# Reading a turned block from its bank, and writing expert results to token slots

## The chip, the cores and the metric

The kernel runs on one core of a Trainium2 chip. The metric is the device time of one launch in microseconds, here the median of three runs: 1955.56 us (1953.64 to 1967.84). PE is TensorE (matmuls, PEld its weight loads), DVE is VectorE, ACT is ScalarE, POOL is GpSimd, SP is SyncE. ACT and DVE read and write PSUM and SBUF; POOL issues the indirect DMAs and SP the plain ones.

## The reference, cut to what matters

Four layers, each a gated cross attention and a gated feed-forward part, work on x of 8 x 256 tokens with 256 features. Three of the four feed-forward parts (layers 0, 1, 3) route every token to two of eight experts. The one that most of the change is about is the last:

```python
def _L3_ffn_ref(x, gate_w, gate_bias, w1, w3, w2, sw1, sw3, sw2):
    scores = softmax(xt @ gate_w.T);  _, idx = top_k(scores + gate_bias, 2)
    weights = take_along_axis(scores, idx, axis=1)
    for e in range(8):
        gate_e = sum(where(idx == e, weights, 0.0), axis=1)
        h = silu(xt @ w1[e].T) * (xt @ w3[e].T)
        y = y + gate_e[:, None] * (h @ w2[e].T)
    z = silu(xt @ sw1.T) * (xt @ sw3.T) @ sw2.T      # two shared experts' width
    return (y + z).reshape(shape)
x = x + tanh(g_ffn[3]) * _L3_ffn_ref(_layernorm(x), ...)
```

Layers 0 (gelu, one shared expert) and 1 (relu, none) have the same form with biases. Layer 2's feed-forward part is not routed.

## The kernel before

**Routed layer.** `find_rows` picks the two experts of each of the 2048 tokens, sorts the 4096 pairs by expert into blocks of 256 rows (`BLOCKS` = 23, the rest is padding), and makes two tables: `token_of`, from a row of a block to its token, and `rows`, from a pair (token, choice) to its row. `routed_experts` then works block by block.

For each block b: POOL gathers its 256 token rows from the DRAM tensor `normed_x` with two indirect DMAs of 128 rows (L1673) into `block_rows`; PE turns them (four transposes, L1719) into PSUM bank 6 or 7; ACT copies the bank to `block_T` in full precision (L1784) and to `block_h`, rounded (L1785); DVE subtracts the two into `block_l` (L1893), the low part. The weights w1 and w2 are split the same way into high and low parts. PE makes the hidden products with three terms (L1699), 24 matmuls of 256 columns for a unit of 512 hidden columns; ACT and DVE make the hidden values and their high and low parts; PE makes the result products (L1709), 12 matmuls in layer 3, whose silu-gated unit is 256 wide, 24 in the others. The result is taken from its banks into `result`, which has two buffers, by ACT in layer 3 (L1601) and by DVE in layers 0 and 1 (L1604), and SP stores it to the DRAM tensor `sorted_y` (L1645), 256 KB.

**Order.** Each engine has its own hand-written queue, and `run` unrolls the first and the last bodies and loops over the ones between. PE's body(b) is: hidden products of b+1, turn of b+2, result products of b. ACT's body(b) in layer 3 is: silu of b, `take(b+1)` (the two copies), high part of the hidden values, high part of w1 (b+2), result of b-1, high part of w2 (b+1). DVE's is: `gated` (silu times the other half, L1849), `split_block(b+1)` (the low part), low parts of the hidden values, of w1 and of w2. In layers 0 and 1 DVE rounds the hidden values and subtracts their low part ahead of `split_block`. PE turns a block only when the low part of the block two before is made, or, before the change, when its high part is.

**Tail of layer 3.** Four batches' shared experts are computed beside the routing (HEAD), four after the blocks (TAIL), two units each: 16 hidden matmuls (L1699) and 8 result matmuls (L1709) a unit. PE runs one unit ahead: the hidden products of unit j+1 come before the result products of unit j, which need unit j's `gated` values from DVE. Meanwhile POOL waits for the last store to `sorted_y`, then issues 32 indirect gathers (L1686) of 128 rows, one for each of 16 tiles and two choices, into a ring of 16 pieces of the w1 buffers. DVE adds each to x with its gate (`combine`, L1937), in groups: after the shared result of batch 4 (L1855) it does 4, after batch 5 it does 8, after batch 6 it does 8 and after batch 7 the last 12. `store_output` (L1658) stores a batch of x when its combines and its shared result are done.

Of the kernel before, what the change touches and what calls it, by code (L numbers as in the profile page):

```python
# [18 lines left out]
I32 = mybir.dt.int32  # L19
# [90 lines left out]
def build(nc, dram, out, stages):  # L110
    with ExitStack() as whole:

        in_use = []

        def sem(name):
            in_use.append(nc.alloc_semaphore(name=name))
            return in_use[-1]

        def clear_semaphores():

            nc.clear_and_free_semaphores(in_use)
# [22 lines left out]
        codes = resident("codes", [P, 2 * TILES])  # L144
# [6 lines left out]
        env = dict(nc=nc, context_w=context_w, homes=homes, dram=dram, sem=sem, psum=psum, x=x, ident=ident, half=half, zero=zero, half32=half32, ctxT=ctxT, tg=tg,  # L151
                   rank=rank, stats=stats, mv=mv, var=var, rstd=rstd, before=before, ones=ones, counting=counting,
                   marks=marks, codes=codes)
        if any(kind == "f" and FFN[n].get("routed") for kind, n in stages):
            env["normed_x"] = nc.dram_tensor("normed_x", (TOKENS, D), F32, kind="Internal").ap()
            env["sorted_y"] = nc.dram_tensor("sorted_y", (BLOCKS * BLOCK, D), F32, kind="Internal").ap()
        env["context_ready"] = False
        env["out"] = out
        env["g_all"] = g_all
        attentions, expert_layers = stages[0::2], stages[1::2]  # L160
        assert all(kind == "a" for kind, n in attentions) and all(kind == "f" for kind, n in expert_layers)
        for (_, a), (_, f), following in zip(attentions, expert_layers, [n for kind, n in attentions[1:]] + [None]):
            with ExitStack() as pair:
                front = front_part(env, pair, f)
                with ExitStack() as scope:
                    attention_layer(env, scope, a, front)
                clear_semaphores()
                with ExitStack() as scope:
                    ffn_layer(env, scope, f, following, front)
                clear_semaphores()  # L170
            env["context_ready"] = True
# [770 lines left out]
def ffn_layer(env, scope, n, following, front):  # L942
# [8 lines left out]
    if routed:  # L951
        t["xn_all"] = front["xn_all"]
        t["gates"] = sb("gates", [P, TILES, cfg["experts"]])
        t["rows"] = sb("rows", [P, 2 * TILES], I32)
# [14 lines left out]
    with nc.Block() as block:  # L969
        @block.sync  # L970
        def _(sp):
            r_sync(sp)
            e_sync(sp)
            if ahead:
                t["operands_left"](sp)
                ahead["load_late"](sp)
            else:
                t["store_output"](sp)
# [75 lines left out]
def find_rows(env, scope, n, t):  # L1054
# [8 lines left out]
    def sb(nm, shape, dt=F32):  # L1063
# [3 lines left out]
        "consts", "chain", "shifted", "exped", "coded", "same", "summed", "table_done", "chosen", "counted",  # L1067
# [18 lines left out]
    t.update({k: sems[k] for k in ("rows_done", "blocks_done", "table_done")}, exponentials=choose.exponentials)  # L1086
# [31 lines left out]
    def place_rows(dve, step):  # L1118
# [29 lines left out]
        nc.vector.tensor_copy(t["rows"][:], rows_f[:].rearrange("p k t -> p (k t)")).then_inc(sems["rows_done"], 1)  # L1148
# [101 lines left out]
def experts(env, scope, n, t):  # L1250
# [205 lines left out]
    t.update(operands_left=operands_left, banks_left=banks_left, stated=stated, rows_places=rows_places)  # L1456
# [14 lines left out]
def routed_experts(env, scope, n, t):  # L1471
# [9 lines left out]
    xs, ys = env["normed_x"], env["sorted_y"]  # L1481
# [12 lines left out]
    COMBINED = (1, 7) if shared == 1 else (4, 12, 20)  # L1494
# [5 lines left out]
    own = own_follows(n)  # L1500
    RING = 8 if own else 16
# [16 lines left out]
    block_T = [sb(f"block_T{s}", [P, DC, BLOCK]) for s in range(2)]  # L1518
# [6 lines left out]
    gathered = [w1[j // 4][:].rearrange("p c i -> p (c i)")[:, j % 4 * D:(j % 4 + 1) * D] for j in range(RING)]  # L1525
# [33 lines left out]
    def run(engine, body):  # L1559
# [3 lines left out]
        for b in range(DEPTH):  # L1563
            body(b, 0, b, max(DEPTH, 3))
        with engine.Fori(1, rounds) as i:
# [42 lines left out]
    def sync(sp):  # L1608
        if own:
            t["ahead"]["load_early"](sp)  # L1610
        for s in range(2):
            sp.dma_start(ys[s * BLOCK:s * BLOCK + P, :], env["ctxT"][:, 0, 0:D]).then_inc(sems[f"stored{s}"], 16)

        def weights(b, s, freed):
# [3 lines left out]
            for u, unit in enumerate(units):  # L1618
# [3 lines left out]
                sp.dma_start(w1[k][:], dram[f"{name}_w1"][unit]).then_inc(sems[f"w_in{k}"], 16)  # L1622
                sp.dma_start(w2[k][:], dram[f"{name}_w2"][unit]).then_inc(sems[f"w_in{k}"], 16)
# [26 lines left out]
        run(sp, body)  # L1650

# [12 lines left out]
    def gpsimd(pool):  # L1664
# [3 lines left out]
        for b in range(BLOCKS):  # L1668
# [7 lines left out]

        for s in range(2):
# [14 lines left out]
    def tensor(pe):  # L1692
# [192 lines left out]
    def vector(dve):  # L1885
# [43 lines left out]
        def combine(j):  # L1929

            tile, k = divmod(j, 2)
            dve.wait_ge(sems[f"gathered{j % RING}"], 16 * (j // RING + 1))
# [4 lines left out]
            nc.vector.scalar_tensor_tensor(x[:, tile, :], gathered[j % RING],  # L1937
# [26 lines left out]
        for k, b in enumerate(TAIL):  # L1964
# [29 lines left out]
    def banks_left(pe):  # L1994
        pe.wait_ge(sems["hidden_out"], UNITS * OUT + HIDDEN0)
        pe.wait_ge(sems["result_out"], RESULTS + RESULT0)
        pe.wait_ge(sems["turned_out"], BLOCKS + 2)

    t.update(operands_left=operands_left, banks_left=banks_left, stated=stated, rows_places=rows_places)
# [137 lines left out]

# [741 lines left out]
```

## Time and profile before

| what | us |
|---|---|
| median of three runs | 1955.56 |
| the profiled execution, and its span | 1955.66, 1953.9 |
| PE busy, DVE busy, ACT busy, POOL busy | 1734.4, 1263.3, 974.7, 528.9 |
| blocks of layer 0 (first gather to last gather's end) | 207.4 to 359.6 |
| blocks of layer 1 | 808.6 to 1044.4 |
| blocks of layer 3 (first turn to last result) | 1760.6 to 1892.3 |
| tail of layer 3 (shared units after the blocks, to the end) | 1891.6 to 1953.9 |

The span runs from the first to the last instruction of the core. The execution's own time lies 1.8 us above it. Busy times of engines overlap; what an engine's work costs is read from whether another engine's queue stood still for it.

### The profile page before, as it was taken

The numbers are of one execution on the slowest core, as the hardware profiler recorded it, in microseconds if no ns is written. First come the engines' busy times: TensorE is split into PE (matmuls) and PEld (weight loads), VectorE is DVE, ScalarE is ACT, GpSimd is POOL, SyncE is SP. The second block draws the span as 40 slices with busy tenths as digits, with TensorE's granted clock in tenths as the row PEclk, the third lists the DMA queues.
The fourth block names the chain that finished last, engine by engine and source line by source line (L and its number), as shares of the span: only waits on it lengthen the run. The fifth ranks groups of instructions, "written<-read, shape, count | busy, mean of one in ns | idle before, by whom it ended". The sixth has DMA issues, their size and how long they took to land. (4 is left out here: it accounts for less than half of the span.)

```text
span 1953.9 us, 32441 instructions
## 1 busy us (share of the span) xinstructions
PE 1734.4 (89%) x11744; PEld 1436.2 (74%) x11744; DVE 1263.3 (65%) x2312; ACT 974.7 (50%) x1739; POOL 528.9 (27%) x492
## 2 busy tenths in 40 slices
PE   6998899987799997599999969999699699798896
PEld 4667799932577776599999648887588466588885
DVE  6886488646355563588888557665545688656644
ACT  4652366523676772277777225444353355316750
POOL 2320343264333332122221450000200244203334
PEclk9998799998799997599999979999699999889998
DMA  3003378520100000567676240000000100025743
GB/s 112 15 20 105 126 254 257 148 79 0 50 1 12 7 12 25 195 217 245 232 233 217 65 130 1 1 1 1 28 1 11 48 12 12 31 76 177 238 148 110
DMA packets 97907, 178.64 MB, mean 91 GB/s; under 512 B 25888, under 2 KB 62650, under 8 KB 96682
## 3 DMA queue, kind: packets, MB, share of 16 engines
q1 hardware_dynamic: 86264, 146.32, 22.8%
q0 software_dynamic: 11232, 30.69, 5.4%
q8 instruction: 76, 1.25, 0.3%
q14 instruction: 47, 0.39, 0.1%
q10 hardware_dynamic: 288, 0.00, 0.0%
HBM read 149.70 MB, written 27.26 MB: 91 GB/s over the span
## 5 line engine op out<-in xcount | busy, mean ns | idle before, releaser
L1673 POOL DMA_INDIRECT f_block_rows_home<-normed_x,f_token_of_sb x138 | 168.6, 1221 | 452.3 <-PE psum L1719 325.8
L1699 PE MATMUL psum<-f_block_h_sb,f_w1h_home 128*128 128x256 f32 x736 | 211.4, 287 | 29.8 <-DVE f_block_l_sb L1893 12.0
L1699 PE MATMUL psum<-f_block_h_sb,f_w1l_home 128*128 128x256 f32 x736 | 206.9, 281 | 0.0
L1699 PE MATMUL psum<-f_block_l_sb,f_w1h_home 128*128 128x256 f32 x736 | 206.8, 281 | 0.0
L2322 PE MATMUL psum<-a_xT_home,context_w 128*128 128x256 f32 x704 | 181.2, 403 | 13.6 <-PEq L122 9.7
L1709 PE MATMUL psum<-f_w2h_home,f_hidden_h_home 128*128 128x256 f32 x644 | 187.4, 291 | 1.8 <-DVE f_result_sb L1604 0.9
L1709 PE MATMUL psum<-f_w2h_home,f_hidden_l_home 128*128 128x256 f32 x644 | 181.8, 282 | 0.0
L1709 PE MATMUL psum<-f_w2l_home,f_hidden_h_home 128*128 128x256 f32 x644 | 181.7, 282 | 0.0
L1699 PEld LDWEIGHTS psum<-f_block_h_sb,f_w1h_home 128*128 128x128 f32 x736 | 141.0, 192 | 38.1 <-issue 28.2
L2487 ACT ACTIVATE a_probsT_sb<-psum 77x1024 f32<-77x1024 f32 (+1 forms) x128 | 130.8, 1022 | 71.4 <-PE psum L2374 69.0
L2322 PEld LDWEIGHTS psum<-a_xT_home,context_w 128*128 128x128 f32 x704 | 131.6, 197 | 45.0 <-issue 20.0
L1801 ACT ACTIVATE f_hidden_sb<-psum,f_b_sb 128x256 f32<-128x256 f32 x276 | 115.7, 471 | 78.2 <-PE psum L1699 76.7
L2374 PE MATMUL psum<-identity,a_probs_sb 128*77 128x128 f32 (+1 forms) x1024 | 141.7, 280 | 11.4 <-DVE a_inv_sb L2662 9.1
L2374 PEld LDWEIGHTS psum<-identity,a_probs_sb 128*77 128x77 f32 (+1 forms) x1024 | 116.1, 142 | 47.2 <-DVE a_inv_sb L2662 19.2
L2414 PE MATMUL psum<-a_wo_sb,a_attT_sb 128*128 128x256 f32 x640 | 145.3, 383 | 2.6 <-ACT a_attT_sb L2509 1.4
L1699 PEld LDWEIGHTS psum<-f_block_l_sb,f_w1h_home 128*128 128x128 f32 x736 | 141.1, 192 | 0.0
L1699 PEld LDWEIGHTS psum<-f_block_h_sb,f_w1l_home 128*128 128x128 f32 x736 | 140.8, 191 | 0.0
L2414 PEld LDWEIGHTS psum<-a_wo_sb,a_attT_sb 128*128 128x128 f32 x640 | 120.2, 192 | 19.1 <-ACT a_attT_sb L2509 2.3
L1686 POOL DMA_INDIRECT f_w_sb<-sorted_y,f_rows x96 | 93.1, 970 | 129.7 <-DMA sorted_y<-f_result_sb 95.3
L1709 PEld LDWEIGHTS psum<-f_w2h_home,f_hidden_h_home 128*128 128x128 f32 x644 | 122.8, 191 | 2.7 <-DVE f_hidden_l_home L1893 2.6
L1709 PEld LDWEIGHTS psum<-f_w2l_home,f_hidden_h_home 128*128 128x128 f32 x644 | 123.0, 191 | 0.0
L1709 PEld LDWEIGHTS psum<-f_w2h_home,f_hidden_l_home 128*128 128x128 f32 x644 | 122.8, 191 | 0.0
(310 smaller groups left out, 3929.8 us busy)
## 6 DMA issues: line engine op xcount, KB each, us to landing
f_w_sb<-in_f_w SPq DMA_DIRECT2D x161, 512.0 KB, 4.8
sorted_y<-f_result_sb SPq DMA_DIRECT2D x69, 256.0 KB, 2.3
normed_x<-f_xn_all SPq DMA_DIRECT2D x24, 256.0 KB, 2.1
f_b_row_sb<-in_f_b SPq DMA_DIRECT2D x46, 128.0 KB, 3.6
f_w_sb<-in_f_w SPq DMA_DIRECT2D x23, 256.0 KB, 4.0
f_block_rows_home<-normed_x,f_token_of_sb POOLq DMA_INDIRECT x138, 4.2
residual<-in_x SPq DMA_DIRECT2D x8, 256.0 KB, 6.2
context_w<-in_a_wk SPq DMA_DIRECT2D x2, 1024.0 KB, 5.2
```

What stands on the lines that cost most here:

```text
L1673: nc.gpsimd.indirect_dma_start(block_rows[b % 2][:, h, :], None, xs, bass.IndirectOffsetOnAxis(ap=column, axis=0)).then_inc(sems[f"rows_in ...
L1686: nc.gpsimd.indirect_dma_start(gathered[j % RING], None, ys, bass.IndirectOffsetOnAxis(ap=t["rows"][:, col:col + 1], axis=0)).then_inc(sem ...
L1699: last = nc.tensor.matmul(hid_ps(q)[:, m, :], w, rhs, start=(j == 0), stop=(j == len(parts) - 1))
L1709: last = nc.tensor.matmul(y_ps[h], v, w, start=(begin and j == 0), stop=(end and j == len(parts) - 1))
L1801: nc.scalar.activation(hidden[q][:, m, :], hid_ps(q)[:, m, :], func, bias=bias[:, 0, m:m + 1]).then_inc(sems["hidden_out"], 1)
L2322: last = nc.tensor.matmul(bank[:, s * SEQ:(s + 1) * SEQ], w[:, k, c * P:(c + 1) * P], xT[:, k, b * SEQ:(b + 1) * SEQ], start=(k == 0), sto ...
L2374: last = nc.tensor.transpose(psum[0:keys, 4 + part, h * P:(h + 1) * P], probs[g % 2][:, 4 * part + h, :], ident[:])
L2414: last = nc.tensor.matmul(bank[:, tile * D:(tile + 1) * D], attT[:, c, tile * P:(tile + 1) * P], wo[:, c, :], start=(c == 0), stop=(c == N ...
L2487: nc.scalar.activation(probsT[h % 2][:, :, tile * P:(tile + 1) * P].rearrange("p (a h) k -> p a h k", a=2), psum[0:keys, 4:6, :].rearrange ...
```

## The change

Three things are changed.

1. In all three routed layers `block_T` and ACT's copy into it are gone; DVE's subtraction reads the full values from the PSUM bank. PE turns a block into a bank only when the low part, not the high part, of the block two before is made.
2. In layer 3 the results are no longer stored in sorted order by SP and gathered by POOL at the end. POOL writes each block's result with two indirect DMAs straight to a DRAM tensor `slots`, where each (choice, token) has its row; rows of padding go to rows of their own behind these (`slot_of`, `unfilled`, `pads`). POOL's order is now gather(b+4), scatter(b). ACT may overwrite a result buffer when its two scatters have landed. After the last scatter SP loads 16 plain pieces of 256 KB (one batch and choice each) into buffers that are free then, all at once.
3. In layer 3's tail the combines are moved between the `gated` operations: none, 2, 8, 14, 20, 26, 32, 32 are done after gated 0 to 7, and none stands after the last shared result.

The loops are unrolled over four blocks instead of `DEPTH` at the start (this differs in layer 1 alone). Layer 3 computes no `rows` table; `slot_of` costs three small DVE operations in its place, and one more at the kernel's start makes `pads`.

```diff
@@ find_rows
+        if direct:
+            step.did(nc.vector.tensor_scalar(unfilled[:], source[:], 0.0, None, ALU.is_equal))
         step.then(nc.vector.tensor_scalar(source[:], source[:], -1.0, 0.0, ALU.add, ALU.max))
         step.then(nc.vector.tensor_scalar(wrapped[:], source[:], float(TOKENS), -float(TOKENS), ALU.is_ge, ALU.mult))
         nc.vector.tensor_tensor(t["token_of"][:], source[:], wrapped[:], ALU.add).then_inc(sems["table_done"], 1)
+        if direct:
+            step.then(nc.vector.tensor_tensor(unfilled[:], unfilled[:], env["pads"][:], ALU.mult))
+            nc.vector.tensor_tensor(t["slot_of"][:], source[:], unfilled[:], ALU.add).then_inc(sems["slots_done"], 1)
@@ routed_experts
-    block_T = [sb(f"block_T{s}", [P, DC, BLOCK]) for s in range(2)]
...
+    BETWEEN = (0, 2, 8, 14, 20, 26, 32, 32)
+    own, direct = own_follows(n), t["direct"]
+    LEAD = 4
...
+    pairs = [v[:, c, :].rearrange("p (h d) -> p h d", d=D) for v in w1[0:2 if own else len(w1)] for c in range(DC)]
+    if direct:
+        pairs += [v[:, k:k + BT, :] for v in w2 for k in range(0, HC, BT)] + [v[:] for v in result]
+        pairs += [v[:].bitcast(F32).rearrange("p c (h d) -> p (c h) d", d=D) for v in block_h]
+    RING = min(len(pairs), 2 * NBATCH) if direct else len(pairs) * BT
@@ take_result
-        engine.wait_ge(sems[f"stored{s % 2}"], uses(i, s) * 16 + STORED0)
+        if not direct:
+            engine.wait_ge(sems[f"stored{s % 2}"], uses(i, s) * 16 + STORED0)
+        elif not (isinstance(b, int) and b < 2):
+            engine.wait_ge(sems[f"stored{s % 2}"], uses(i, s) * (16 * BT))
@@ sync
-            sp.wait_ge(sems["result_out"], b + (R0 + 1 + RESULT0))
-            sp.dma_start(ys[bass.ds(b * BLOCK, BLOCK), :].rearrange("(h p) d -> p h d", p=P),
-                         result[s % 2][:]).then_inc(sems[f"stored{s % 2}"], 16)
+            if not direct:
+                ...
+        if direct:
+            for s in range(2):
+                sp.wait_ge(sems[f"stored{s}"], 16 * BT * len(range(s, BLOCKS, 2)))
+            for j in range(RING):
+                load_slots(sp, j)
+
+    def load_slots(sp, j):
+        b, k = divmod(j, 2)
+        first = k * TOKENS + b * SEQ
+        sp.dma_start(pairs[j % RING], slots[first:first + SEQ, :].rearrange("(h p) d -> p h d", p=P)).then_inc(
+            sems[f"gathered{j % RING}"], 16)
@@ gpsimd
+        def scatter(b):
+            pool.wait_ge(sems["result_out"], b + (R0 + 1 + RESULT0))
+            for h in range(BT):
+                column = t["slot_of"][:, b * BT + h:b * BT + h + 1]
+                nc.gpsimd.indirect_dma_start(slots, bass.IndirectOffsetOnAxis(ap=column, axis=0),
+                                             result[b % 2][:, h, :], None).then_inc(sems[f"stored{b % 2}"], 16)
+        if direct:
+            for b in range(4):
+                gather(b)
+            pool.wait_ge(t["slots_done"], 1)
+            for b in range(BLOCKS):
+                if b + 4 < BLOCKS:
+                    gather(b + 4)
+                scatter(b)
...
+            return
@@ tensor, turn
-            pe.wait_ge(sems["turned_out"], b + 1)
+            pe.wait_ge(sems["block_low"], b + 1)
@@ scalar, take
-            nc.scalar.activation(block_T[s][:], turn_ps(s), ACT.Copy)
             nc.scalar.activation(block_h[s][:], turn_ps(s), ACT.Copy).then_inc(sems["turned_out"], 1)
@@ vector
-            low(block_l[s], block_T[s], block_h[s], "block_low")
+            nc.vector.tensor_tensor(block_l[s][:], turn_ps(s), block_h[s][:].bitcast(F32), ALU.subtract).then_inc(
+                sems["block_low"], 1)
...
+        for k, b in enumerate(TAIL if silu else []):
+            v0 = U0 + BLOCKS * per_expert + k * shared
+            for u in range(shared):
+                gated(dve, v0 + u, (v0 + u) % 2)
+                if u == 0 and k:
+                    dve.wait_ge(sems["result_out"], R0 + BLOCKS + k + RESULT0)
+                until = BETWEEN[k * shared + u]
+                for j in range(combined, until):
+                    combine(j)
+                combined = until
+            if combined:
+                dve.wait_ge(sems["combined"], combined)
+            shared_result(dve, b, v0)
```

## Rows read from the trace of the kernel before

**Rows 1.** The page, busy time of each engine over the span.
```profile
PE 1734.4 (89%) x11744; PEld 1436.2 (74%) x11744; DVE 1263.3 (65%) x2312; ACT 974.7 (50%) x1739; POOL 528.9 (27%) x492
```
**Rows 2.** Busy time by stretch: blocks of layer 0, of layer 1, of layer 3.
```profile
core 0: us, PE busy (x) PEld busy (x) DVE busy (x) ACT busy (x) POOL busy (x), PEclk, DMA share, GB/s
245.00:360.00 115.00, 109.15 (x890) 105.78 (x889) 92.58 (x104) 80.22 (x137) 45.84 (x35) 1.00 0.81 255
820.00:1060.00 240.00, 239.91 (x2054) 239.71 (x2053) 198.14 (x205) 173.01 (x290) 51.31 (x39) 1.00 0.72 236
1797.00:1853.00 56.00, 49.56 (x404) 47.58 (x403) 38.17 (x51) 41.70 (x72) 21.02 (x21) 1.00 0.74 237
```
**Rows 3.** PE's waits in layer 3, 1775 to 1885: total, times, longest us.
```profile
PE psum L1699 <- DVE f_block_l_sb L1893: 7.7, 12, 0.7
PE psum L1699 <- issue: 4.8, 9, 0.5
```
**Rows 4.** PE's waits in layer 0, 245 to 358.
```profile
PE psum L1699 <- DVE f_block_l_sb L1893: 4.3, 12, 0.4
```
**Rows 5.** Timeline of one block of layer 3: start, us, what, idle before and releaser.
```profile
1838.67 0.69 DVE L1849 TENSOR_TENSOR f_hidden_sb<-f_silus_sb,psum 128x512 f32<-128x512 f32 x1 [0.56 <-PE psum L1699]
...
1839.11 0.60 ACT L1784 ACTIVATE f_block_T_sb<-psum 128x512 f32<-128x512 f32 x1 [1.20 <-PE psum L1719]
...
1839.60 0.59 ACT L1785 ACTIVATE f_block_h_sb<-psum 128x512 fp32r<-128x512 f32 x1
...
1840.23 0.69 DVE L1893 TENSOR_TENSOR f_block_l_sb<-f_block_T_sb,f_block_h_sb 128x512 fp32r<-128x512 f32 x1 [0.87 <-ACT f_block_h_sb L1785]
...
1841.16 0.38 PE L1699 MATMUL psum<-f_block_h_sb,f_w1h_home 128*128 128x256 f32 x1 [0.67 <-DVE f_block_l_sb L1893]
...
1841.55 0.60 ACT L1601 ACTIVATE f_result_sb<-psum 128x512 f32<-128x512 f32 x1
```
**Rows 6.** Timeline of one block of layer 0, DVE's low parts.
```profile
297.07 1.23 DVE L1893 TENSOR_TENSOR f_hidden_l_home<-f_hidden_sb,f_hidden_h_home 128x1024 fp32r<-128x1024 f32 x1
...
298.21 0.69 DVE L1893 TENSOR_TENSOR f_block_l_sb<-f_block_T_sb,f_block_h_sb 128x512 fp32r<-128x512 f32 x1
```
**Rows 7.** Timeline of POOL: indirect DMAs, the time to make one and the gap.
```profile
1895.19 0.95 POOL L1686 DMA_INDIRECT f_w_sb<-sorted_y,f_rows  x1 [20.43 <-DMA sorted_y<-f_result_sb]
...
1839.35 0.94 POOL L1673 DMA_INDIRECT f_block_rows_home<-normed_x,f_token_of_sb  x1 [3.01 <-PE psum L1719]
1840.60 1.15 POOL L1673 DMA_INDIRECT f_block_rows_home<-normed_x,f_token_of_sb  x1 [0.30 <-issue]
...
1764.46 1.44 POOL L1673 DMA_INDIRECT f_block_rows_home<-normed_x,f_token_of_sb  x1 [0.30 <-issue]
...
224.09 1.96 POOL L1673 DMA_INDIRECT f_block_rows_home<-normed_x,f_token_of_sb  x1 [0.30 <-issue]
```
**Rows 8.** DMA issues, count, median us to landing: layer 3's blocks, then its tail.
```profile
f_block_rows_home<-normed_x,f_token_of_sb POOLq DMA_INDIRECT x37, 3.8
...
f_w_sb<-sorted_y,f_rows POOLq DMA_INDIRECT x32, 2.8
```
**Rows 9.** Chain that ended last, tail of layer 3: start, us, what.
```profile
1891.64 6.91 PE psum L1699 x32
1898.55 1.73 PE psum L1709 x8
...
1937.26 5.42 PE psum L1709 x16
1942.70 0.76 DVE residual L1855
```
**Rows 10.** PE's waits in the tail, 1890 to 1954.
```profile
PE psum L1709 <- DVE f_hidden_sb L1849: 5.3, 2, 2.6
```
**Rows 11.** Busy time of the tail's last matmuls (columns of rows 2).
```profile
1937.20:1942.70 5.50, 5.40 (x16) 4.19 (x16) 0.60 (x2) 0.00 (x0) 0.44 (x1) 0.69 0.29 92
```
**Rows 12.** Timeline of DVE, the last combines.
```profile
1943.49 6.96 DVE L1937 SCALAR_TENSOR_TENSOR residual<-f_w_sb,f_chosen_gates,residual 128x256 f32<-128x256 f32 x12
```

More of the change, by code:

```diff
@@ L953, in ffn_layer @@
         t["gates"] = sb("gates", [P, TILES, cfg["experts"]])
[L954 removed]
+        t["rows"] = sb("rows", [P, 2 * TILES], I32) if n != 3 else None
         t["chosen_gates"] = sb("chosen_gates", [P, 2, TILES])
@@ L1066, in find_rows @@
     sems = {k: env["sem"](f"{name}_{k}") for k in (
-        "consts", "chain", "shifted", "exped", "coded", "same", "summed", "table_done", "chosen", "counted",
+        "consts", "chain", "shifted", "exped", "coded", "same", "summed", "table_done", "slots_done", "chosen", "counted",
         "rows_done", "blocks_done")}
@@ L1492, in routed_experts @@
     SUMS_AT = FIRST - 1 if shared == 1 else 5
-    COMBINED = (1, 7) if shared == 1 else (4, 12, 20)
+    COMBINED = (1, 7)
+    BETWEEN = (0, 2, 8, 14, 20, 26, 32, 32)
     gate, zero = env["tg"][:, 4 + n:5 + n], env["zero"][:]
@@ L1523, in routed_experts @@
     result = [sb(f"result{s}", [P, BT, D]) for s in range(2)]
-    gathered = [w1[j // 4][:].rearrange("p c i -> p (c i)")[:, j % 4 * D:(j % 4 + 1) * D] for j in range(RING)]
+    pairs = [v[:, c, :].rearrange("p (h d) -> p h d", d=D) for v in w1[0:2 if own else len(w1)] for c in range(DC)]
[3 more added lines that the diff above has]
+    RING = min(len(pairs), 2 * NBATCH) if direct else len(pairs) * BT
+    gathered = [pairs[j // BT][:, j % BT, :] for j in range(RING)] if not direct else None
     def rows_places(attention):
@@ L1562, in run @@
         rounds = (BLOCKS - max(DEPTH, 3)) // DEPTH
-        for b in range(DEPTH):
-            body(b, 0, b, max(DEPTH, 3))
-        with engine.Fori(1, rounds) as i:
+        for b in range(LEAD):
+            body(b, b // DEPTH, b % DEPTH, max(DEPTH, 3))
+        with engine.Fori(LEAD // DEPTH, rounds) as i:
             for s in range(DEPTH):
@@ L1610, in sync @@
             t["ahead"]["load_early"](sp)
-        for s in range(2):
+        for s in range(0 if direct else 2):
             sp.dma_start(ys[s * BLOCK:s * BLOCK + P, :], env["ctxT"][:, 0, 0:D]).then_inc(sems[f"stored{s}"], 16)
@@ L1622, in weights @@
                 sp.dma_start(w1[k][:], dram[f"{name}_w1"][unit]).then_inc(sems[f"w_in{k}"], 16)
+                if freed and direct and not silu and u == per_expert - 1:
+                    sp.wait_ge(sems["result_out"], (b - DEPTH) + (R0 + 1 + RESULT0))
                 sp.dma_start(w2[k][:], dram[f"{name}_w2"][unit]).then_inc(sems[f"w_in{k}"], 16)
@@ L1643, in body @@
             what = weights(b + DEPTH, s, True) if ahead >= DEPTH else None
-            sp.wait_ge(sems["result_out"], b + (R0 + 1 + RESULT0))
-            sp.dma_start(ys[bass.ds(b * BLOCK, BLOCK), :].rearrange("(h p) d -> p h d", p=P),
-                         result[s % 2][:]).then_inc(sems[f"stored{s % 2}"], 16)
+            if not direct:
+                sp.wait_ge(sems["result_out"], b + (R0 + 1 + RESULT0))
+                sp.dma_start(ys[bass.ds(b * BLOCK, BLOCK), :].rearrange("(h p) d -> p h d", p=P),
+                             result[s % 2][:]).then_inc(sems[f"stored{s % 2}"], 16)
             if what:
@@ L1650, in sync, with slots_left @@
         run(sp, body)
+        if direct:
[8 more added lines that the diff above has]
+            sems[f"gathered{j % RING}"], 16)
+    def slots_left(sp):
+        for j in range(RING if direct else 2 * NBATCH, 2 * NBATCH):
+            b, k = divmod(j - RING, 2)
+            sp.wait_ge(sems["combined"], (b * TPB + TPB - 1) * 2 + k + 1)
+            load_slots(sp, j)
     def store_output(sp):
@@ L1667, in gpsimd, with gather @@
         pool.wait_ge(t["table_done"], 1)
-        for b in range(BLOCKS):
+        def gather(b):
             if b >= 2:
@@ L1675, in gpsimd @@
                                                  sems[f"rows_in{b % 2}"], 16)
+        def scatter(b):
[4 more added lines that the diff above has]
+                                             result[b % 2][:, h, :], None).then_inc(sems[f"stored{b % 2}"], 16)
+        if direct:
+            for b in range(4):
[5 more added lines that the diff above has]
+                scatter(b)
+            rows = t["ahead"]["rows"] if t["ahead"] and t["ahead"]["between"] else None
+            for b in range(NBATCH if rows else 0):
+                rows["power"](pool, b, batch_tiles(b))
+            return
+        for b in range(BLOCKS):
+            gather(b)
         for s in range(2):
@@ L1931, in combine @@
             tile, k = divmod(j, 2)
-            dve.wait_ge(sems[f"gathered{j % RING}"], 16 * (j // RING + 1))
+            if direct:
+                pair = tile // TPB * 2 + k
+                dve.wait_ge(sems[f"gathered{pair % RING}"], 16 * (pair // RING + 1))
+                row = pairs[pair % RING][:, tile % TPB, :]
+            else:
+                dve.wait_ge(sems[f"gathered{j % RING}"], 16 * (j // RING + 1))
+                row = gathered[j % RING]
             if j:
@@ L2136, in _ @@
             step.then(nc.vector.tensor_scalar(position[:], counting[:, P:P + 1], 1.0, None, ALU.add))
+            step.then(nc.vector.tensor_scalar(env["pads"][:], marks[:, 0:2 * BLOCKS], float(2 * TOKENS - 1), position[:],
+                                              ALU.add, ALU.add))
             step.then(nc.vector.tensor_scalar(codes[:], counting[:, 0:2 * TILES], float(P), position[:], ALU.mult, ALU.add))
```

29 lines of the change are left out of this document (17 added, 12 removed).

## Prediction

> **What bounds the kernel.** I read the page's busy times first: PE is busy 1734.4 of 1953.9 us, DVE 1263.3, ACT 974.7, POOL 528.9 [rows 1]. So a shorter ACT or POOL counts only where PE's queue stands still for it. The busy time by stretch says where that is: layer 1's blocks have no hole (239.91 of 240), layer 0's 5.9 us in 115, layer 3's 6.4 in 56, all at full clock [rows 2]. PE's waits name the cause: in layer 3 it waits before the hidden products 21 times, once a block, 12.5 us in all, for `block_l` or for "issue" right behind it [rows 3]; in layer 0 it waits for `block_l` as well, 0.4 us at most [rows 4]. Last the chain that ended last, for the tail: PE runs the shared units from 1891.64, but twice waits 2.6 us for `gated`, which DVE does only after a group of combines [rows 9, 10]; after the last matmul the chain goes through the shared result and 12 combines of DVE [rows 9, 12].
>
> **Part 1, `block_T` away, layer 3.** The timeline of one block [rows 5] shows a chain: turn done about 1839.08, `block_T` at 1839.11, `block_h` at 1839.60, `block_l` from 1840.23 to 1840.92, and PE, idle for 0.67, starts at 1841.16. PE's own work between turn and that start, the result products, ended 0.67 earlier, at 1840.49. Without `block_T` the rest moves ahead by 1839.60 - 1839.11 = 0.49 us: PE could start at 1840.67. The wait falls from 0.4 to 0.7 down to at most 0.2. 21 blocks x 0.49 = 10.3 us; the two bounds are 0 (if another operand is late next) and all 12.5 us of the waits. I take 10.3 since the operands next in line have room: the low part of w1 for this start was made a block earlier, `gated` (1838.67) and `block_l` don't overlap on DVE, and ACT and DVE are busy 41.7 and 38.2 of 56 us [rows 2], so they follow a block 0.5 us shorter (a block is about 56 / (404 matmuls / 40) = 5.55 us now, PE's share 4.9).
>
> DVE now reads PSUM for one input. Rows price this: `gated` reads SBUF and PSUM and takes 0.69, `block_l` from two SBUF tiles 0.69 [rows 5]; cost nothing. The Trainium skill (Perfetto Trace Analysis, Optimizing Scalar/DVE Operations) gives about 60 ns of access overhead on SBUF and 125 on PSUM; by that, as an estimate, `block_l` would be 0.065 us longer, 1.4 us over the 21 blocks. The trace does not agree, so I leave it out.
>
> **Layers 0 and 1.** In layer 0 `block_l` stands behind `hidden_l` on DVE (297.07 to 298.30, then 298.21 [rows 6]), and `hidden_l` behind the gelus, not behind ACT's copies; taking `block_T` away moves nothing. In layer 1 PE has no hole. Both 0. Bounds: -4.3 us (layer 0's waits) to +0.06 x 21 = +1.3, should the PSUM read cost one small step. PE's new wait on the low part before a turn is always met: the hidden products just ahead of that turn in PE's queue need a later block's low part. The four unrolled blocks of layer 1 cost nothing visible while PE is full.
>
> **Part 2, stores become scatters.** SP loses 23 stores that nobody on the path waited for, and with them the wait for each result, so weights can only be asked for earlier. POOL gains 46 indirect DMAs beside the 38 gathers it mixes with them. The trace has no scatter. The nearest rows: a gather from `sorted_y` takes 0.95, in the blocks 0.94 and 1.15, with 0.30 between two [rows 7]; bounds 0.94 and 1.96 us. I take 0.95 to 1.0, as 128 rows of 1 KB are the same work with source and target changed about. POOL's block is then 4 x 0.30 + 0.94 + 1.15 + 2 x 0.95 = 5.2 us against PE's new 5.55 - 0.49 = 5.06. It looks bound, but has slack: gather(b+4) begins right after turn b+2 and is needed at turn b+4, two blocks (10.1 us) later; its second DMA is issued about 1.5 us after the turn and lands 3.8 later [rows 7, 8], at 5.3 to 5.6, so POOL may lag 4.5 us. A scatter can't begin until the result is out (ACT's copy at 1841.55 + 0.60, 3.1 us after the turn [rows 5]), and its buffer is wanted two blocks later, with the same slack. At 5.2 the lag grows by 19 x 0.14 = 2.7 us, hidden. After gather 22 there are only scatters, so POOL catches up.
>
> The DVE operations at the table (one of 0.2 us ahead of `token_of`) lie beside PE's HEAD products, which run on long after the first gathers landed; `pads` is one small operation at the start. Both nothing.
>
> **Part 3, tail.** The last result leaves as before, about 1892.3 on the old clock of times. Two scatters (2.2 us), landing 2.8 to 3.8 after the second's issue [rows 7, 8]: about 1897.5. SP then issues 16 loads of 256 KB. At the 237 GB/s that layer 3's blocks moved [rows 2] one comes every 1.1 us, the first some 2.5 to 4 us on: piece 0 at about 1901, piece 15 at 1918. DVE needs pieces 0 and 1 by about 1907 before PE would feel it (PE's third result products begin at 1908.9 and need shared result 4 and gated 2), and piece 15 not before 1926. So the data is in time, and no `gated` is late: between two `gated` DVE has 6 combines of 0.58 = 3.5 us and at most one shared result of 0.76, in 5.2 us of PE. PE runs the eight units without a hole: 8 x (6.91 / 2 + 1.73) = 41.5 us [rows 9], from 1891.64 to 1933.1. Now the result products end at 1942.70: two waits of 2.65, and matmuls at a granted clock of 0.69 after them (16 in 5.42 us for 3.46) [rows 9, 11]. That is 9.6 us. Behind the last shared result the 12 combines, 6.96 + 0.04, go as well [rows 12]. The last store stays (1950.45 to 1953.9). Sum: -16.6 us. Bounds: 0 to -17.
>
> **Sum.** 1955.66 - 10.3 - 16.6 = 1928.8 us. The profiled execution lies 0.1 us over the median 1955.56, so both are the same base.
>
> **Rivals.**
> *POOL holds the blocks back, some.* The rows show indirect DMAs of 1.44 where two of DVE's two-input operations ran [rows 7]. With 1.44 for each scatter POOL's block is 0.94 + 1.15 + 2.88 + 1.2 = 6.17 us, the lag grows 1.1 a block, 19 x 1.11 = 21 us less the 4.5 of slack = +16.6: 1945. For: POOL will now ask in every phase of DVE's block. Against: `block_l` leaves the operations that read two SBUF tiles, and the scatters begin when the low part of w1 is nearly done. The Trainium skill (SBUF — State Buffer, Who interferes with whom) has the rule: a DVE instruction with two SBUF inputs and a GpSimd one that reads SBUF exclude each other, and the later one blocks in full. By that rule the 1.15 and 1.44 are waits for the DVE operation in flight, and each of the four index reads can meet one.
> *No gain in the blocks, or late pieces in the tail.* If another operand is as late as `block_l`, only the tail counts: 1939. If the pieces landed 5 us later than reckoned, PE would wait once for 1 to 2 us and run slow for as long: about 1932.
> *Slower.* One mechanism: scatters that take as long as the longest gather seen, 1.96 [rows 7]. POOL's block is 7.2 us, 19 x 2.15 - 4.5 = +36 on 1929: 1965; with 1.96 for the gathers too, 9.0 us, 19 x 3.98 - 4.5 = +71: 2000. It is slower than before from 19 x (s - 5.06) - 4.5 > 26.9, a POOL block s of 6.7 us, scatters of 1.7 each. Against: of the gathers in layer 3's blocks none is longer than 1.44.
> *The change does not do what it says:* not to be seen; the same products are made.
>
> **Numbers.** As predicted, 1924 to 1935: 0.72. POOL holds back, 1935 to 1955: 0.14. Blocks or tail give only a part, 1934 to 1942: 0.09. Slower: 0.05, of which 0.03 by over 1%. The range is 1922 to 1943: below it 0.04, above it about 0.13. This kernel's measurement tells 1%, 19.6 us, from nothing. Faster by over 1% is below 1936: 0.74; within 1%: 0.23; slower: 0.03.
>
> **What the new profile would show.** PE's wait before the hidden products in layer 3 at most 0.2 us a block, and PE busy 97% there; ACT has no L1784; `block_l` still 0.69; scatters of 0.95 to 1.15 us; POOL without long idle in layer 3's blocks; layers 0 and 1 as before to 2 us; the tail's 192 matmuls without a wait and at full clock; the last DVE operation a shared result, some 41 us after the last block. I am wrong if PE waits for gathered rows, or ACT for landed scatters, or if layer 3's blocks still take 5.5 us.

## The result, and the profile after

The changed kernel takes 1940.97 us (median of 14 runs, 1933.95 to 1952.88) against 1955.91 of the kernel before (14 runs beside it): ratio 0.9918, 95% interval 0.9901 to 0.9935. A second set gave 0.9926 (0.9904 to 0.9948). It is faster, by 15 to 16 us where 27 were forecast; 1929 was forecast, within 1922 to 1943. That is 0.8%, so within the 1% to which the forecast gave 0.23. The profiled execution took 1940.14 us, its span 1938.3.

The page's busy times, and busy time by stretch (blocks of layer 0, of layer 1, of layer 3), answer to [rows 1, 2]:

```profile
PE 1734.1 (89%) x11744; PEld 1436.9 (74%) x11744; DVE 1265.3 (65%) x2315; ACT 942.5 (49%) x1670; POOL 549.3 (28%) x506
```
```profile
245.00:360.00 115.00, 109.17 (x891) 105.75 (x891) 92.11 (x103) 70.37 (x119) 46.02 (x35) 1.00 0.82 252
820.00:1060.00 240.00, 237.79 (x2014) 237.20 (x2015) 193.60 (x201) 160.15 (x265) 55.73 (x44) 0.98 0.71 237
1797.00:1853.00 56.00, 51.76 (x403) 49.49 (x404) 38.98 (x51) 37.45 (x62) 43.81 (x41) 0.97 0.72 238
```

ScalarE fell by 32 us and POOL rose by 20. In layer 3's 56 us PE gained only 2.2 us of busy time and made 403 matmuls as before (404), so its blocks run at nearly the old rate. PE's waits there, 1775 to 1885 (total, times, longest), answer to [rows 3]; the last line is ScalarE's wait in the same stretch:

```profile
PE psum L1784 <- DMA f_block_rows_home<-normed_x,f_token_of_sb: 4.2, 4, 2.3
PE psum L1764 <- DVE f_block_l_sb L1961: 1.2, 7, 0.2
PE psum L1764 <- issue: 1.2, 3, 0.9
```
```profile
ACT f_result_sb L1623 <- DMA slots<-f_result_sb,f_slot_of_sb: 4.2, 4, 1.9
```

The 12.5 us for `block_l` and "issue" became 2.4, as forecast. In their place PE waits for gathered rows, one time for 2.3 us, and ScalarE for landed scatters. After the long wait the granted clock falls, and 40 matmuls run in 6 us, where 447 in 56 us (the kernel with more buffers, called deep below, with 1.3 us idle) make 48:

```profile
1833.74 0.66 PE L1784 MATMUL psum<-identity,f_block_rows_home 128*128 128x128 f32 x4 [2.30 <-DMA f_block_rows_home<-normed_x,f_token_of_sb]
```
```profile
1835.00:1841.00 6.00, 6.00 (x40) 6.00 (x40) 3.90 (x5) 3.56 (x7) 4.57 (x5) 0.72 0.67 226
```

This fall costs the blocks nothing in the end. A second profile of the same kernel (e6) has no wait over 1.2 us and full clock throughout, and its blocks take the same 124.6. PE from 1780 to 1890, first profile and second (us, busy and count, granted clock, DMA share, GB/s):

```profile
1780.00:1890.00 110.00, 102.94 (x814) 0.98 0.67 216
```
```profile
1780.00:1890.00 110.00, 101.69 (x813) 1.00 0.69 223
```

POOL's indirect DMAs from 1785 to 1875, by line (count, busy, mean ns, idle before), answer to [rows 7]:

```profile
L1725 POOL DMA_INDIRECT slots<-f_result_sb,f_slot_of_sb x33 | 37.3, 1131 | 10.1 <-issue 10.1
L1717 POOL DMA_INDIRECT f_block_rows_home<-normed_x,f_token_of_sb x32 | 33.6, 1051 | 9.8 <-issue 9.4 <-PE psum L1784 0.3
```

POOL has only 0.30 between two instructions and next to no wait: it is the bound, as e3, e5 and e7 below bear out. From 1781.62 to 1877.14 it does 17 blocks in 95.5 us, 5.62 each. The tail answers to [rows 9, 10, 12]: PE's one wait in it, the first loads of slots on SP's queue, and DVE's last operations:

```profile
PE psum L1774 <- DVE f_hidden_sb L1913: 0.7, 1, 0.7
```
```profile
1896.35 7.07 SPq L1686 DMA_DIRECT2D f_w_sb<-slots  x12
```
```profile
1930.93 0.48 DVE L2008 SCALAR_TENSOR_TENSOR residual<-f_block_h_sb,f_chosen_gates,residual 128x256 f32<-128x256 f32 x1 [0.49 <-DVE residual L2008]
1931.33 0.68 DVE L1913 TENSOR_TENSOR f_hidden_sb<-f_silus_sb,psum 128x512 f32<-128x512 f32 x1
1934.17 0.75 DVE L1919 SCALAR_TENSOR_TENSOR residual<-psum,tg,residual 128x512 f32<-128x512 f32 x1 [2.16 <-PE psum L1774]
```

Nothing follows the last shared result; the 12 combines behind it are gone. Layer 0 waits for `block_l` as before [rows 4]:

```profile
PE psum L1764 <- DVE f_block_l_sb L1961: 4.3, 12, 0.4
```

To compare kernels I split each profiled span at two marks: PE's first product of layer 3's first block, and its first product of the shared units behind the last block. Between them lie 23 blocks, 23 x 5.06 = 116.4 us if PE alone sets the pace (5.06 is the prediction's; the deep kernel's blocks come out at it).

| kernel | blocks of layer 3 | shared units to end of span | span |
|---|---|---|---|
| before | 1765.18 to 1891.48: 126.30 | 62.42 | 1953.9 |
| after | 1766.90 to 1891.53: 124.63 | 46.77 | 1938.3 |
| bank only | 1765.40 to 1882.52: 117.12 | 60.68 | 1943.2 |
| slots only | 1765.89 to 1892.47: 126.58 | 46.83 | 1939.3 |
| half of the gathers | 1772.82 to 1889.56: 116.74 | 46.84 | 1936.4 |
| deep, rows and results | 1769.32 to 1885.72: 116.40 | 46.48 | 1932.2 |
| after, again | 1770.64 to 1895.25: 124.61 | 46.85 | 1942.1 |
| short low parts | 1767.16 to 1885.65: 118.49 | 46.85 | 1932.5 |
| deep rows alone | 1770.74 to 1899.90: 129.16 | 46.40 | 1946.3 |
| bank, sorted, between | 1767.12 to 1884.31: 117.19 | 51.39 | 1935.7 |
| deep results alone | 1766.37 to 1892.03: 125.66 | 46.47 | 1938.5 |
| deep, again | 1768.00 to 1884.66: 116.66 | 46.44 | 1931.1 |

The expectations of the first four experiments count the blocks from the first turns, 3.9 us earlier, so their 128.5 is the table's 124.6 and their 120 its 116.1. One execution of the deep kernel took 6334.56 us; no profile of it was kept, and its ratio is worked out without it. The two kernels that were profiled twice repeat their blocks within 0.3 us and their tail within 0.1; the time ahead of the first mark moves by up to 8 us between kernels.

### The profile page after: what moved, and what is told of

The parts are those of the page before. It is cut to its first block and busy times, and to the rows that moved or that the text cites. A ratio compares the mean times of both kernels' runs of the same rounds, so it can differ in the third digit from the quotient of the medians.

```text
span 1938.3 us, 32286 instructions
## 1 busy us (share of the span) xinstructions
PE 1734.1 (89%) x11744; PEld 1436.9 (74%) x11744; DVE 1265.3 (65%) x2315; ACT 942.5 (49%) x1670; POOL 549.3 (28%) x506
## 5 line engine op out<-in xcount | busy, mean ns | idle before, releaser
L1957 DVE TENSOR_TENSOR f_w1l_home<-f_w_sb,f_w1h_home 128x1024 fp32r<-128x1024 f32 x92 | 112.2, 1220 | 12.0 <-ACT f_w1h_home L1886 7.2
```

The source lines that it names most:

```text
L1957: nc.vector.tensor_tensor(out[:], whole[:], part[:].bitcast(F32), ALU.subtract).then_inc(sems[sem], 1)
```

## The experiments

The theory: part 1 does free PE, but POOL, with two more indirect DMAs a block, lengthened by waits for DVE's operations in flight, is slower than PE and takes the gain back. The rivals: part 1 buys nothing by itself; the longer POOL times have another cause; the result buffers hold PE, not the rows.

**Each part alone (e1, e2).** Bank only: `block_T` goes, the stores to `sorted_y` and the old tail stay. Slots only: the changed kernel with `block_T` put back:

```
# e1, on the kernel before
-            nc.scalar.activation(block_T[s][:], turn_ps(s), ACT.Copy)
...
-            low(block_l[s], block_T[s], block_h[s], "block_low")
+            nc.vector.tensor_tensor(block_l[s][:], turn_ps(s), block_h[s][:].bitcast(F32), ALU.subtract).then_inc(
+                sems["block_low"], 1)
...
# e2, on the changed kernel: the same edit undone
```

> The first part of the change alone: block_l comes from the PSUM bank and block_T is gone in every layer; the results still go to sorted_y by a store of SP, and the tail stays as before. Theory A: after the change PE in layer 3 is no longer held by block_l, but the eight-odd per cent of extra work on POOL (two scatters a block, each lengthened by a two-input op of DVE in flight) holds the blocks instead; without the scatters POOL has two gathers a block, 2 x 1.4, and 5.06 a block is PE's. So the stretch from POOL's first gathers' turn to the first shared unit, 130.2 before and 128.5 after the change, falls to about 120, and the run to about 1945 to 1947. Theory B: the bank read buys nothing in itself, because another operand is as late as block_l was: the stretch stays at 128 to 130 and the run at about 1955. Both: layers 0 and 1 as before, the tail from the first shared unit to the end of the span 62.2, as before.

> The second and third part of the change alone: results to token slots by indirect DMA in layer 3 and the combines between its shared gates; ScalarE's copy of the turned block and the low part from that copy are kept in all layers. Theory A (POOL bounds layer 3's blocks after the change at about 5.6 a block, about the 5.5 that block_l's lateness gave before): the stretch of layer 3's blocks stays within 2 of the 128.5 of the changed kernel, the tail falls by 15.6, and the run is about 1940 to 1942, so that the first part is worth next to nothing beside the second. Theory B (the first part did give its 10 and something else took it, the scatters' writes for instance, additively): the blocks take about 10 longer, 138, and the run is about 1950.

Measured: e1 1947.82 (ratio 0.9945, 0.9923 to 0.9967), blocks 117.12; e2 1944.54 (0.9934, 0.9913 to 0.9956), blocks 126.58. PE's waits, 1775 to 1885, in e1 and in e2:

```profile
PE psum L1698 <- issue: 1.1, 4, 0.7
PE psum L1698 <- DVE f_block_l_sb L1895: 1.1, 6, 0.2
PE psum L1708 <- DVE f_hidden_l_home L1891: 0.8, 1, 0.8
```
```profile
PE psum L1765 <- DVE f_block_l_sb L1959: 7.6, 12, 0.7
PE psum L1765 <- issue: 4.3, 8, 0.6
```

Alone, part 1 shortens the blocks by 9.2 us (10.3 forecast) and leaves PE 3 us of waits. Theory A holds for it and theory B falls. Its tail is 1.7 shorter too (60.68 against 62.42): the last 16 result products take 3.72 at full clock, where before they took 5.42 at 0.69 [rows 11], behind a wait of 2.63 in both [rows 10]. Bank only's last products:

```profile
1928.31 3.72 PE L1708 MATMUL psum<-f_w2s,f_hidden_sb 128*128 128x256 f32 x16 [2.63 <-DVE f_hidden_sb L1847]
```

In e2 `block_l` is late as before [rows 3] and POOL's load costs 0.3. So part 1 is worth 9.2 without scatters and 2.0 with them (126.58 against 124.63): the two parts aren't additive, and the scatters cost 7.5 once PE could go faster. Both medians lie 1 to 3 us above what theory A gave for the runs.

**POOL's load (e3).** The second gather of each block from the fifth on is left out:

```
-            for h in range(BT):
+            for h in range(1 if direct and b >= LEAD else BT):
...   # and PE's turn waits for one landed piece less
```

> The changed kernel, but in layer 3 each block from the fifth on gathers only its first 128 rows; the second half of the buffer keeps the rows of an earlier block, so those rows' results are not the reference's. POOL then issues three indirect DMAs a block there and not four. Theory A (POOL's throughput bounds the blocks): 3 x (1.10 + 0.30) = 4.2 a block is under PE's 5.06, so the blocks run at about 5.1, the stretch of layer 3's blocks falls from 128.5 to about 119 to 121, and the run is at about 1931. Theory B (the blocks are held by something else, the weights' DMA, the clock, or ScalarE's wait for landed scatters, which stay two a block): no change, the stretch 127 to 129, the run about 1940.

Measured: 1935.76 (0.9888, 0.9846 to 0.9929), blocks 116.74. With three indirect DMAs a block PE sets the pace, with the scatters in place. That names POOL's queue, not the scatters' writes. It halves the gathers' reads as well, but e5 and e7 below keep every transfer and come to 116.4 and 118.5. The run is 5 over the expected 1931, and the time ahead of the blocks is 6 longer than in the changed kernel's profile.

**What lengthens them (e7).** The low parts of w1 and w2, DVE's operations with two SBUF inputs, cut to 16 columns:

```
-                    low(w1l[q], w1[unit_later(i, s, u, 2)[1]], w1h[q], "w1_low")
+                    if direct and not begins(b):
+                        some = slice(0, 16)
+                        raw1 = w1[unit_later(i, s, u, 2)[1]]
+                        nc.vector.tensor_tensor(w1l[q][:, 0, some], raw1[:, 0, some], w1h[q][:, 0, some].bitcast(F32),
+                                                ALU.subtract).then_inc(sems["w1_low"], 1)
...   # and so for w2l
```

> The changed kernel, but in layer 3, after the first block, the low parts w1l and w2l are subtracted in 16 columns only and not in 1024, so the rest of them is old data and the results are not the reference's. DVE's two-input operations of 1.22 and 0.6 nearly vanish there; POOL's four indirect DMAs a block stay. Theory A with the lock (an indirect DMA of POOL takes 0.96 to 1.00, and longer by what is left of a two-SBUF-input operation of DVE that is in flight when it begins): POOL's indirect DMAs between 1785 and 1875 fall from a mean of 1.10 to at most 1.00, its pace from 5.62 to about 5.15 a block, and the blocks from 124.6 to 117 to 119, the run to 1932 to 1935. Theory B (the longer ones have another cause, the landing transfers of the weights for instance): POOL's mean stays at 1.10 and the blocks at 124 to 125.

Measured: 1932.38 (0.9863, 0.9825 to 0.9901), blocks 118.49. POOL's indirect DMAs from 1785 to 1875:

```profile
L1725 POOL DMA_INDIRECT slots<-f_result_sb,f_slot_of_sb x36 | 36.6, 1015 | 11.0 <-issue 11.0
L1717 POOL DMA_INDIRECT f_block_rows_home<-normed_x,f_token_of_sb x34 | 33.8, 995 | 10.4 <-issue 10.4
```

All four are still there, and each costs about 1.0 where after had 1.13 and 1.05: the blocks lose 6.1 us. DVE has less to do as well (25.5 busy in the 56 us, for 39.0), but what PE had lost stood on gathered rows, not on DVE. The timelines of the changed kernel show the single case (start, us):

```profile
1786.02 0.69 DVE L1961 TENSOR_TENSOR f_block_l_sb<-psum,f_block_h_sb 128x512 fp32r<-128x512 f32 x1 [0.32 <-ACT f_block_h_sb L1849]
1786.30 0.99 POOL L1725 DMA_INDIRECT slots<-f_result_sb,f_slot_of_sb  x1 [0.31 <-issue]
1787.49 1.23 DVE L1957 TENSOR_TENSOR f_w1l_home<-f_w_sb,f_w1h_home 128x1024 fp32r<-128x1024 f32 x1 [0.18 <-ACT f_w1h_home L1886]
1787.59 1.99 POOL L1717 DMA_INDIRECT f_block_rows_home<-normed_x,f_token_of_sb  x1 [0.30 <-issue]
```
```profile
1835.07 0.69 DVE L1961 TENSOR_TENSOR f_block_l_sb<-psum,f_block_h_sb 128x512 fp32r<-128x512 f32 x1 [1.68 <-ACT f_block_h_sb L1849]
1835.21 0.96 POOL L1717 DMA_INDIRECT f_block_rows_home<-normed_x,f_token_of_sb  x1 [0.30 <-issue]
```

The gather at 1787.59 begins 0.10 after `w1l` and takes 1.99: the 1.13 that `w1l` has left, and 0.86. The one at 1835.21 begins inside the new `block_l`, which reads one operand from PSUM, and takes 0.96. Before, one that began inside the old `block_l` took 1.15 [rows 7]. The Trainium skill (SBUF — State Buffer, Who interferes with whom) says that a DVE instruction with two SBUF inputs contends with a GpSimd instruction that reads SBUF, and that one with at most one SBUF input, outside the 2-port perf modes, does not; both rows agree.

All 64 indirect DMAs that begin between 1785 and 1875 in the changed kernel bear this out. Of them, 39 begin outside such a DVE operation and take 0.96 to 1.00 each, also the 16 that begin inside a DVE operation that reads PSUM for one input. The 25 that begin inside one with two SBUF inputs take 1.27 on average, up to 1.99; where it has over 0.15 left, each takes what is left and 0.84 to 0.87, but for one that begins 0.02 after `hidden_l` and takes 0.96. The other way round nothing shows: the 14 `w1l` that begin during an indirect DMA take 1.22 to 1.25, the three others 1.23.

**More slack (e5, e8, e10, e11).** e5 has four row and four result buffers in layer 3 in the place of two, and gathers six blocks ahead; e8 only the rows, e10 only the results:

```
+    NR = 4 if direct else 2
+    LEAD = 8 if direct else 4
+    AHEAD = 6
...
+        block_rows = block_rows + [sb(f"more_rows{s}", [P, BT, D]) for s in range(2)]
...
-    result = [sb(f"result{s}", [P, BT, D]) for s in range(2)]
+    result = [sb(f"result{s}", [P, BT, D]) for s in range(NR)]
...
-            if b >= 2:
-                pool.wait_ge(sems["turned"], b - 1)
+            if b >= NR:
+                pool.wait_ge(sems["turned"], b - NR + 1)
```

> The changed kernel with four row buffers and four result buffers in layer 3 in the place of two each, and gathers issued six blocks ahead in the place of four. The same number of indirect DMAs. Theory A1 (the order and waits on POOL's queue, a gather that waits for a turn ahead of a scatter that could go, make up much of the 5.62 a block): with the slack of two more blocks at the start and fewer waits, POOL's pace is 4 x (1.10 + 0.30) = 5.6 at the worst and 5.2 at the best, and two blocks more of slack (2 x 5) cover 21 x 0.5; the stretch of layer 3's blocks falls from 128.5 to about 119 to 122, the run to about 1931 to 1933. Theory A2 (POOL's throughput is the bound and the slack is used up all the same at the end, since the last scatter and the slots behind it don't wait for anything but POOL): the blocks fall by the slack alone and the first slot load comes as late as now, so that the tail waits for it: run 1936 to 1940. Theory B (not POOL): 1940, stretch unchanged.

> Of the kernel with four row and four result buffers (blocks 116.4, as PE alone needs) only the row buffers: four of them, gathers six blocks ahead, results in two buffers. Theory A (POOL's lateness reached PE through the gathered rows, 4.2 in 4 waits; the slack that counts is in rows gathered ahead): the blocks take 117 to 119, and ScalarE waits for landed scatters instead without holding PE; run 1932 to 1934. Rival (the result buffers hold it: ScalarE waits for a landed scatter before it takes the next result, and PE's bank and the next block_h stand behind it): the blocks stay at 122 to 125; run 1937 to 1941.

> Of the kernel with four row and four result buffers only the result buffers: results in four, rows in two, gathers four blocks ahead as in the changed kernel. With rows alone in four the blocks took 129.2 against 124.6, ScalarE waited 24.4 in 13 for landed scatters, and PE behind it. Theory C (both paths carry POOL's lateness to PE, the results' sooner): without the wait for landed scatters POOL may lag by what two row buffers give, some 4, of the 23 x (5.5 - 5.06) = 10 that it falls behind if nothing holds it; what is over comes through the gathered rows: blocks 119 to 122, run 1934 to 1938. Theory D (the result buffers are all of it): blocks 116.4 to 117.5 as with both, run 1930 to 1933.

> The kernel with four row and four result buffers once more, in more rounds, as the version to recommend. Blocks 116.4 and the tail 46.5 again; the run within 1928 to 1933, 0.985 to 0.988 of the kernel before.

Measured: e5 1930.04 (0.9862, 0.9814 to 0.9910), blocks 116.40; again in e11 1933.07 (0.9872, 0.9849 to 0.9894), blocks 116.66. Its busy time by stretch and its last scatter:

```profile
1797.00:1853.00 56.00, 54.72 (x447) 52.62 (x446) 42.41 (x56) 40.38 (x66) 43.64 (x41) 1.00 0.76 251
```
```profile
1889.67 0.97 POOL L1730 DMA_INDIRECT slots<-f_result_sb,f_slot_of_sb  x1 [0.30 <-issue]
```

447 matmuls in 56 us at full clock, and PE needs nothing from POOL any more. POOL is no faster (1.11 a DMA from 1785 to 1875, with the same 0.30 between, so theory A1's shorter POOL block did not come): it ends its last scatter at 1890.64, 4.9 after PE began the shared units, which don't need it yet. The lag is hidden, not removed. Each half alone fails. e8 takes 1946.33 (0.9941), blocks 129.16; e10 1942.01 (0.9921), blocks 125.66. The fences are e8's POOL from 1785 to 1875, its ScalarE and its PE from 1755 to 1885, and e10's PE from 1755 to 1890:

```profile
L1730 POOL DMA_INDIRECT slots<-f_result_sb,f_slot_of_sb x29 | 31.7, 1094 | 8.8 <-issue 8.8
L1722 POOL DMA_INDIRECT f_block_rows_home<-normed_x,f_token_of_sb x16 | 21.7, 1359 | 4.9 <-issue 4.9
L1722 POOL DMA_INDIRECT f_more_rows_sb<-normed_x,f_token_of_sb x14 | 18.6, 1330 | 4.3 <-issue 4.3
```
```profile
ACT f_result_sb L1628 <- DMA slots<-f_result_sb,f_slot_of_sb: 24.4, 13, 2.5
```
```profile
PE psum L1769 <- DVE f_block_l_sb L1969: 7.0, 7, 1.0
```
```profile
PE psum L1787 <- DMA f_block_rows_home<-normed_x,f_token_of_sb: 6.8, 9, 1.2
```

With deep rows POOL's lateness reaches PE through the results: ScalarE waits for a landed scatter, its `block_h` of the next turn and DVE's `block_l` come late behind it, and PE waits for `block_l`. With deep results it reaches PE through the rows. I expected 117 to 119 of e8 and 119 to 122 of e10, and the rival 116.4 to 117.5 of e10; all were wrong. e8's rival was right in kind, but its blocks came out 4.5 longer than the changed kernel's: its gathers took 1.34 on average, because 14 of 30 began inside a DVE operation with two SBUF inputs (1.76 on average), where in the changed kernel 5 of 32 did. Why they fall so wasn't tried.

**The tail without scatters (e9).** Bank only, with the combines between the shared gates and the gathers from `sorted_y` kept:

```
+    BETWEEN = (0, 5, 7, 13, 16, 21, 24, 27)   # combines done after gated 0 to 7; 5 left for the end
```

> Block_l from the bank, results by SP's store to sorted_y as before, no scatters; POOL gathers the results in the tail as before, but the combines stand between the shared gates as in the changed kernel, as far as the gathers can have landed: 27 of the 32, and 5 behind the last shared result. Theory A (the gain of the tail is the interleaving's, and the scatters only buy the last few combines): blocks 117.1 as with the bank alone, from the first shared unit to the last shared result 43.4 as in the changed kernel, then 5 x 0.58 and 3.4 of store: run 1932 to 1935. Rival (POOL's 32 gathers at 1.26 each are too slow for it: the combines wait between the gates and PE for them): 3 to 8 more, run 1936 to 1941.

Measured: 1939.20 (0.9904, 0.9875 to 0.9933), blocks 117.19, from the first shared unit to the last shared result 42.46. PE waits for nothing in the tail. DVE's last operations:

```profile
1926.80 1.66 DVE L1937 SCALAR_TENSOR_TENSOR residual<-f_w_sb,f_chosen_gates,residual 128x256 f32<-128x256 f32 x3
1928.73 0.48 DVE L1937 SCALAR_TENSOR_TENSOR residual<-f_w_sb,f_chosen_gates,residual 128x256 f32<-128x256 f32 x1 [0.26 <-DMA f_w_sb<-sorted_y,f_rows]
1930.28 0.48 DVE L1937 SCALAR_TENSOR_TENSOR residual<-f_w_sb,f_chosen_gates,residual 128x256 f32<-128x256 f32 x1 [1.07 <-DMA f_w_sb<-sorted_y,f_rows]
```

The last gathers arrive late by 0.26 and 1.07, and the end is 4.6 us after the changed kernel's (51.39 against 46.77). The median is 4 above the expected 1932 to 1935, and lies in the rival's 1936 to 1941; but the rival's mark, waits of PE between the gates, is not there, and 4 is within what the front moves. So of the tail's 15.7 us the interleaving gives 9.3 (bank only's 60.68 to 51.39), the scatters 4.6, and 1.7 is the clock under the last products, which bank only has back without either; in the blocks the scatters cost 7.5. The two kernels' times can't be told apart.

**The front (e6).** The changed kernel unaltered:

> The changed kernel once more, unaltered, for a second profile of it. The blocks of layer 3, from PE's first product of the first block to its first shared unit, took 124.6 in its first profile, against 126.3 before; the stretch from the last gather of layer 0 to the first of layer 1 took 456.9 against 450.6, with no edit in it. If POOL holds the blocks, as theory A has it, the 124.6 comes again within 1; if a chance fall of the granted clock made it (it was 0.91 between 1825 and 1845), it comes out near 122 to 123. If the 456.9 is chance it may come out at 451 as well.

Measured: 1942.69, blocks 124.61, so the 124.6 is no accident, and a fall of the clock did not make it. Its front is 3.7 later than in the first profile. Most of what moves it lies between layers 0 and 1, where the change has no edit. PE, 725 to 735, before and after (us, busy and count, granted clock, DMA share, GB/s):

```profile
725.00:730.00 5.00, 4.99 (x47) 1.00 0.01 3
730.00:735.00 5.00, 5.00 (x24) 1.00 0.00 0
```
```profile
725.00:730.00 5.00, 4.80 (x24) 0.57 0.00 0
730.00:735.00 5.00, 5.00 (x29) 0.50 0.02 3
```

The clock falls beside a short hole of PE in both kernels; before, it is whole again from 725 on, and after, it stays at half, 1.2 GHz, up to 735. From the start of layer 0's last gather to that of layer 1's first it is 450.6 to 450.9 in before, e1, e2, e9 and e10 (450.7), and 453.8 to 457.3 in after, e3, e5, e6, e7, e8 and e11. e10 has both parts of the change and the short time, so the edits don't force the long one; what decides between the two stays open. Half of the 6.3 us comes back later: from layer 1's last gather to layer 3's first it is 701.2 before and 698.0 in the first profile after.

## Why the prediction was right and where it failed

The sum can be set against the profile: 1940.14 is 11.3 over 1928.8. Of that 8.6 are the blocks, 1.0 the tail, 1.7 the front.

- *Part 1, -10.3.* Alone it gives -9.2 (e1), by the mechanism named: the wait of PE for `block_l` falls to at most 0.2 each (once 0.7 goes to "issue"), and the PSUM operand is free (`block_l` still 0.69). The 0.065 that the figures of the Trainium skill (Perfetto Trace Analysis, Optimizing Scalar/DVE Operations) would add isn't there.
- *POOL's slack: this step failed.* The prediction put a scatter at 0.95 to 1.0 and POOL's block at 5.2 us, with a lag of 2.7 under a slack of 4.5. The term that was mis-sized is the indirect DMAs' time: four of them at 3.99 us, with the scatters at their clean cost. The clean cost was right (0.97 to 1.00), but in the blocks a scatter takes 1.13 and a gather 1.05 on average (1.09 and 1.12 in e6), 4.36 for the four, and the block 5.62 with the gaps and a few waits. So the lag was not hidden by the slack, and PE waited. With the prediction's own formula, 19 x (5.62 - 5.06) = 10.6 of lag less the 4.5 gives 6.1; measured is 7.5 (124.63 against 117.12). The rate failed; the slack of 4.5 was not measured by itself, but fits within 1.4 us. What happened is the rival "POOL holds the blocks back, some" (0.14) at half its price: it assumed 1.44 a scatter, 16.6 us in all, and gave 1945. The Trainium skill's rule on two SBUF inputs was cited there, and each indirect DMA does pay what the operation in flight has left, though not the other way round; how many of them meet one (25 of 64) could not be read beforehand.
- *What is late next.* The prediction calls itself wrong if PE waits for gathered rows, or ACT for landed scatters, or if layer 3's blocks still take 5.5 us: the first two happened, and the blocks take 124.63 / 23 = 5.42.
- *Part 3, -16.6.* Measured -15.65. PE runs the eight units but for one wait of 0.7, where a combine held a gate.
- *Layers 0 and 1, nothing.* Layer 0's blocks are unchanged (109.17 against 109.15 busy). Layer 1's stretch [rows 2] begins late by the front's 6 us, not through the change's blocks: the windows at 950 to 1060 have 110.00 of 110 busy in both.
- *The front, nothing.* It moved by 1.7 in the profiled execution, and no run shows that the change did it.
- *The range* held the time because it reached for the rivals; the likeliest case's own range, 1924 to 1935, with a chance of 0.72, did not. That the time lies inside 1922 to 1943 is no success of the mechanism in the blocks: there the sum had 10.3 us and the kernel got 1.7.

The best version tried is e5 / e11: 0.9872 (0.9849 to 0.9894), 24 us under the kernel before.

## What to carry to other kernels

When an edit shortens the bound engine's block, compare the new block time with every other engine's block, at durations taken while the others run, and count the lag over all blocks against the slack in buffers. Slack must be deepened on every path by which a slow engine reaches the bound one: here half of it cost 1.0 or 4.5 us in the blocks, and all of it gave 8.2. Test two parts of a change alone and together: here a gain of 9.2 and none (-0.3) in the blocks made 1.7 together.

## What the runs showed of the hardware

An indirect DMA of 128 rows holds POOL for 0.94 to 1.00 us plus 0.30 before the next, a gather and a scatter alike, and up to 1.99 when it begins inside a DVE operation that reads two SBUF tiles; DVE's operation isn't lengthened by it (1.22 to 1.25 for `w1l`). A PE wait of 2.3 us was followed by a granted clock of 0.72 over the next 6 us (1.2 GHz for part of it). Waits of up to 0.7 in the same blocks were not, the granted clock in the kernel before being 1.00 there. A wait of 2.63 in the tail was followed by 0.69 before and by 1.00 in bank only, so the wait's length alone doesn't decide it.
